# A transformer layer with routed experts on one core: all stages rewritten (stacked heads in 64 rows, four buffers a ring, weighted sums on TensorE)

## The reference

```
qkv  = x @ w_qkv                      # 16 heads of 8 numbers each
attn = softmax(causal(q k^T / sqrt(8))) @ v
a    = layernorm(attn @ w_proj + b_proj + x) * gamma + beta
x2   = layernorm(x + a)
p    = softmax(x2 @ gate_w^T); the best 2 of 14 experts, weights p0/(p0+p1), p1/(p0+p1)
moe  = w0 * expert_i0(x2) + w1 * expert_i1(x2)    # expert: gelu(x2 w1 + b1) w2 + b2, 128 -> 256 -> 128
out  = layernorm(x2 + clip(x2 + moe, -100, 100))
```

## Time and profile before

| what | us |
|---|---|
| median of 3 runs (lowest, highest) | 615.03 (613.7, 618.78) |
| span of the profiled execution | 603.8 |
| busy: PE, PEld | 408.8, 311.8 |
| busy: DVE, ACT, POOL | 334.4, 289.7, 329.2 |
| instructions | 13418 |

### The profile page before, as it was taken

One profiled execution on the slowest core, in us unless ns is written; L12 is line 12 of the kernel. 1 busy time (PEld: TensorE's weight loads), 2 busy tenths in 40 slices (PEclk: granted clock), 3 DMA queues, 4 the chain that ended last, 5 costly groups with the idle time before them and its releaser, 6 DMA issues.

```text
span 603.8 us, 13418 instructions
## 1 busy us (share of the span) xinstructions
PE 408.8 (68%) x3651; PEld 311.8 (52%) x3651; DVE 334.4 (55%) x1238; ACT 289.7 (48%) x670; POOL 329.2 (55%) x460
## 2 busy tenths in 40 slices
PE   3178998679779669789879678315778877874000
PEld 2045676557557447556657455214757766863000
DVE  3355687467557557567658554443445444442893
ACT  2015576465466455465546456214444544542563
POOL 3803355475466464465566567642656555553793
PEclk9989999798798798798888889557898889898555
DMA  2658773454354362453363210252222222221462
GB/s 59 68 93 191 149 120 54 61 73 54 53 73 58 49 79 38 60 66 57 66 72 42 41 33 19 82 152 60 70 67 75 66 73 68 77 64 43 140 175 69
DMA packets 78121, 45.39 MB, mean 75 GB/s; under 512 B 11217, under 2 KB 76003, under 8 KB 78076
## 3 DMA queue, kind: packets, MB, share of 16 engines
q1 hardware_dynamic: 72668, 35.22, 33.4%
q0 software_dynamic: 4544, 8.44, 5.0%
q10 hardware_dynamic: 864, 1.19, 0.7%
HBM read 18.61 MB, written 14.28 MB: 54 GB/s over the span
## 4 chain that ended last, share of the span: by engine, by line
SPq 27%; PE 23%; DMA 22%; issue 12%; DVE 8%; ACT 3%; POOL 3%; another core or an unknown queue 0%; POOLq 0%; ACTq 0%; DVEq 0%
DMA k_stack<-part_l 18%; SPq L475 16%; PE M L1140 5%; SPq L507 5%; PE M L1143 3%; PE G L1189 2%; PE M L1325 2%; PE S L1109 2%; SPq L501 2%; PE S L1318 2%; DMA rows<-sorted_rows 2%; DVE row_max L831 1%; DVE probs L1062 1%; DVE stats L1072 1%; PE S L1119 1%
## 5 line engine op out<-in xcount | busy, mean ns | idle before, releaser
L831 DVE TENSOR_REDUCE row_max<-M 128x2 f32<-128x512 f32 (+1 forms) x192 | 129.1, 679 | 88.0 <-PE M L1143 87.4
L676 ACT ACTIVATE probs<-S 128x768 f32<-128x768 f32 x128 | 103.4, 809 | 80.9 <-PE S L1119 70.6
L1140 PE MATMUL M<-k_stack,q_stack 96*128 96x256 bf16 (+1 forms) x512 | 85.9, 279 | 64.3 <-DMA k_stack<-part_l 61.1
L637 POOL DMA_INDIRECT results<-y_rows x78 | 79.8, 1023 | 66.6 <-DVE y_rows L1052 41.1
L1140 PEld LDWEIGHTS M<-k_stack,q_stack 96*128 96x128 bf16 x512 | 44.9, 110 | 84.0 <-DMA k_stack<-part_l 56.2
L583 POOL TENSOR_SCALAR_AFFINE_SELECT probs<-probs 128x256 f32<-128x256 f32 x128 | 49.2, 408 | 67.6 <-ACT probs L676 66.7
L627 POOL DMA_INDIRECT sorted_rows<-x,row_no x64 | 63.2, 987 | 28.0 <-issue 20.7
L1143 PE MATMUL M<-causal_neg,ident_bf 128*128 128x256 bf16 (+1 forms) x192 | 68.2, 355 | 0.0
L1325 PE MATMUL M<-probs,hT 128*128 128x128 f32 x312 | 55.3, 305 | 14.3 <-ACT hT L758 7.2
L758 ACT ACTIVATE hT<-S,probs 128x128 f32<-128x128 f32 x156 | 51.3, 369 | 24.1 <-PE S L1318 19.8
L1318 PE MATMUL S<-rows_t,probs 128*128 128x128 f32 x312 | 57.4, 313 | 0.5 <-ACT rows_t L752 0.2
(11 more groups left out here) (166 smaller groups left out, 795.3 us busy)
## 6 DMA issues: line engine op xcount, KB each, us to landing
rows<-sorted_rows SPq DMA_DIRECT2D x78, 64.5 KB
q_stack<-part_h SPq DMA_DIRECT2D x48, 64.0 KB
k_stack<-part_h SPq DMA_DIRECT2D x48, 64.0 KB
xin<-in_L_attn_target_dram SPq DMA_DIRECT2D x16, 128.0 KB, 3.3
q_stack<-part_m SPq DMA_DIRECT2D x32, 64.0 KB
k_stack<-part_m SPq DMA_DIRECT2D x32, 64.0 KB
xres<-in_L_attn_target_dram SPq DMA_DIRECT2D x16, 128.0 KB, 3.2
q_stack<-results SPq DMA_DIRECT2D x8, 256.0 KB, 3.1
```

Of the source, the lines that this page charges most:

```text
L637: pool.indirect_dma_start(results, bass.IndirectOffsetOnAxis(ap=y_rows[:, q, D:ROW].bitcast(U32), axis=0), y_rows[:, q, 0:D], None, bounds ...
L676: act.activation(probs[:, n], S[n % 2][:, 0:3 * T], ACT.Exp, scale=SCALE).then_inc(exp_done, 1)
L831: dve.tensor_reduce(row_max[:, (r - 1) % 3, h0:h0 + nh, half], M[i % 2][:, :].rearrange("p (h k) -> p h k", h=nh), X, ALU.max).then_inc(m_ ...
L1140: pe.matmul(bank[:, j * keys:j * keys + keys], q_stack[0:SHIFT, b, h0 + j, half * P:half * P + P], k_stack[0:SHIFT, b, h0 + j, 0:keys], st ...
```

## The change

- **Stacks.** Two heads share one slot: one in rows 0 to 63, one in rows 64 to 127 (`TILE` = 64), so 8 slots instead of 16. A part goes to every 8th partition, 16 in all. Matmuls of scores and maxima have 64 rows; the two halves of the array write different PSUM banks, in alternation for scores, unit by unit for maxima. The masks are matmuls of 64 rows too, two per former one, of half the columns each. The shift rows are set to zero by two more DMAs a step and written by two instead of one.
- **Order of the body.** Rings of 4 instead of 3, everything from the maxima on lies one step further behind (maxima for t - 2, scores t - 3, ..., scatter t - 6), 22 steps instead of 21, all written out. `early` is t < 3, where ACT issues the DMAs of k. The first four loads of x stand at the start, the expert weights at t = 4, 5, 6. The shift's turn stands earlier in unit 7.
- **Routing in fewer operations.** One comparison instead of two, no copies of logits, indices and best values, the region's offset added by the rank matmuls, one sum less; the mean's sign and the epsilon of the two layer norms go from DVE to POOL (4 small operations a step).
- **Experts.** All 78 tiles written out with constant counts. Layer 1 is two tiles behind, layer 2 four, bias and scatter five; 3 buffers for turned rows and hidden values, 10 for results. ACT also makes 64 diagonal matrices of the weights, one a tile from tile 6 on.
- **Last stage.** PE puts x2 into 8 PSUM banks (8 matmuls of 512 columns) and adds the weighted results with 8 matmuls of 128 columns a chunk. All 16 loads are issued at once, from rows that lie side by side (2 KB instead of 512 B). DVE's clip reads PSUM; the negative mean's product goes to POOL.

The diff, cut to its core:

```diff
-    SHIFT = 96
+    TILE = P // 2
+    SHIFT = 6
+    R = 4
+    HR = 3
+    YR = 10
...
         def run(eng, body):
-            for t in range(FIRST):
-                body(t, t % 3, t // 3)
-            with eng.Fori(0, (LAST - FIRST) // 3) as i:
...
+            for t in range(B + 6):
+                body(t, t % R, t // R)
...
         def s_unit(t, u):
-            return (t - 2, u - 2) if u >= 2 else (t - 3, u + NP - 2)
+            return (t - 3, u - 2) if u >= 2 else (t - 4, u + NP - 2)
...
# SP, body
-                        for stack, part, which, places in parts:
-                            for n in places:
-                                sp.dma_start(stack[HD * n:HD * n + HD, r], part[:, r, which]).then_inc(stacked[r], 16)
+                    after(sp, s_ready, NP * (t + 1 - R))
+                        for a in range(2):
+                            sp.dma_start(q_stack[TILE * a + SHIFT:TILE * a + SHIFT + 2, r],
+                                         zeros_bf[0:2, None, :].broadcast_to([2, NP, T])).then_inc(stacked[r], 16)
+                    sp.wait_ge(h_split, t + 1)
+                    for n in (0, 1, 3):
+                        sp.dma_start(q_stack[n:P:HD, r], part_h[:, r, 0]).then_inc(stacked[r], 16)
...
+                    for w in range(2):
+                        sp.dma_start(q_stack[SHIFT + w:P:TILE, b], shift_t[w * 2 * NP * TT:(w + 1) * 2 * NP * TT, b]).then_inc(shifted, 16)
...
# PE, scores
-                for j in range(2):
-                    h = 2 * n + j
-                    pe.matmul(S[n % 2][:, j * T:j * T + T], k_stack[:, b, h, 0:P], q_stack[:, b, h, :],
...
+                for half, at, nq in ((0, 0, T), (1, T, P)):
+                    for a in range(2):
+                        rows = slice(TILE * a, TILE * a + TILE)
+                        last = pe.matmul(S[n % 2][:, 512 * a + at:512 * a + at + nq], k_stack[rows, b, n, half * P:half * P + P],
+                                         q_stack[rows, b, n, T - nq:T], start=(half == 0), stop=True, skip_group_check=True)
...
# PE, maxima
+                rows = slice(TILE * a, TILE * a + TILE)
+                bank = M[a]
+                for j in range(ng):
+                    pe.matmul(bank[:, j * keys:j * keys + keys], q_stack[rows, b, g0 + j, half * P:half * P + P],
+                              k_stack[rows, b, g0 + j, 0:keys], start=(j == 0), stop=False, skip_group_check=True)
+                for c in range(2):
...
+                    last = pe.matmul(diag, mask_m[rows, c], ident_fold[rows, None, :].broadcast_to([TILE, ng, TILE]), start=False,
...
# experts
         def run_tiles(eng, body):
+            for s in range(TILES + 5):
                 body(s, s % XR, s // XR)
...
+                if 0 <= n < 2 * NT:
+                    act.activation(diag[:, n], ident[:, :], ACT.Copy, scale=wgt[:, n // 2, n % 2:n % 2 + 1]).then_inc(diag_done, 1)
...
# PE, last stage
+                pe.matmul(acc[c][:, :], ident[:, :], x2_all[:, bass.ts(c, 2), :].rearrange("p b n -> p (b n)"), start=True, stop=False,
...
+                pe.wait_ge(got_in[c], 32)
+                for i in range(CH):
+                    n = CH * c + i
+                    for k in range(2):
+                        last = pe.matmul(acc[c][:, i * D:i * D + D], diag[:, 2 * n + k], got[k][:, n], start=False, stop=(k == 1),
+                                         skip_group_check=True)
+                last.then_inc(acc_done, 1)
```

More of the change, by code:

```diff
@@ L525, in store @@
                 sp.dma_start(out_chunks[c], fin[:, half]).then_inc(out_sent[half], 16)
[L527 removed]
+            run_chunks(sp, (4, store))
             for half in range(2):
@@ L557, in more_constants, with zero_keys @@
+            def zero_keys(some):
+                for i in some:
+                    pool.memset(zeroed(k_stack[:, i]), 0).then_inc(keys_zeroed[i], 1)
+            def more_constants():
                 pool.memset(v_aug[:, :, :, :, HD:32], 0.0).then_inc(consts_p, 1)
@@ new lines, in _ @@
+            for q in range(XR):
+                dve.memset(expert_unit[:, q:q + 1], float(1 << EXPERT_BITS * q)).then_inc(numbered, 1)
+            for q in range(2):
+                dve.memset(block_unit[:, q:q + 1], float(1 << BLOCK_BITS * q)).then_inc(numbered, 1)
+            dve.memset(zeroed(q_stack[:, 1]), 0).then_inc(queries_zeroed[1], 1)
+            dve.wait_ge(consts, 4)
+            for a in range(2):
+                part = slice(TILE * a, TILE * a + TILE)
+                dve.tensor_copy(ident_fold[part, :], ident_bf[part, part]).then_inc(folded, 1)
@@ new lines, in _, with masks_below @@
+            dve.wait_ge(wqk_in, 16)
+            for a in range(2):
+                last = dve.tensor_copy(wqk[:, :, D // 2 * a:D // 2 * a + D // 2].rearrange("p w (d g) -> p w d g", d=HD),
+                                       wqk_raw[:, 0:2 * D].rearrange("p (w g a d) -> p w a d g", w=2, g=NP, a=2)[:, :, a])
+            last.then_inc(consts_v, 1)
+            for i in range(2, R):
+                dve.memset(zeroed(q_stack[:, i]), 0).then_inc(queries_zeroed[i], 1)
+            def masks_below():
+                dve.wait_ge(masks, 8)
+                rows = slice(TILE, P)
+                dve.tensor_copy(mask_m[rows], mask_m1[rows]).then_inc(folded, 1)
+                dve.tensor_copy(mask_s[rows], mask_s1[rows]).then_inc(folded, 1)
+                dve.wait_ge(gate_turned, 1)
+                dve.tensor_copy(gate_t[:, :], M[0][:, 0:E]).then_inc(consts_v, 1)
@@ L1111, in scores @@
[L1111 to L1120 removed]
+                    pe.wait_ge(shifted, 32 * (s + 1))
@@ new lines, in scores @@
+                if n % 2:
+                    for c in range(2):
+                        for a in range(2):
+                            rows = slice(TILE * a, TILE * a + TILE)
+                            diag = S[n % 2][:, 512 * a:512 * a + 2 * T].rearrange("p (k q) -> p k q", k=2)[:, :, TILE * c:TILE * c + TILE]
+                            last = pe.matmul(diag, mask_s[rows, c], ident_fold[rows, None, :].broadcast_to([TILE, 2, TILE]), start=False,
+                                             stop=True, skip_group_check=True)
@@ L1226, in body @@
-                    if u == 2 and isinstance(t, int) and t == B + 3:
+                        if t == 0:
+                            pe.wait_ge(weights_in, 80)
+                            pe.transpose(M[0][:, 0:E], gate_raw[:, :], ident[0:E, 0:E]).then_inc(gate_turned, 1)
+                    if u == 2 and on(t) and not early(t):
+                        project(t, r)
+                    for i in m_units(u) if on(t - 2) else ():
+                        if i == 2 and on(t) and not early(t):
+                            turn_x(t, r, lap)
+                        maxima(t, r, i)
@@ L1228, in body @@
+                    if u == 2 and t == B + 4:
                         pe.wait_ge(seen_done, B)
                         pe.wait_ge(y_ready, B)
[L1230 to L1234 removed]
+                        pe.matmul(G[:, 0:E], ones_bf[:, :], seen[(B - 1) % 2], start=True, stop=True).then_inc(counts_ready, 1)
```

884 lines of the change are left out of this document (443 added, 441 removed).

## The result

The changed kernel takes 535.93 us (median of 4 runs, 531.87 to 541.66), the kernel before 614.37 in the same comparison: a ratio of 0.875, 95% interval 0.866 to 0.884. Forecast were 510, range 478 to 548. The profiled execution took 531.87 us, with a span of 530.1. Medians are of all executions; a ratio with an interval leaves out those that took over 1.5% more than the same kernel's fastest.

A forecast was written before the change was run, and what follows sets the result against it. The prediction took attention to be bound by a loop in which PE waits for the stack DMAs, with PE the next bound. Attention 339, experts 122 and last stage 38 gave 499 us, with 11.2 more 510; range 478 to 548.

The forecast's parts named there:

- (a): Attention: rings of 4 and one step more between stacks and maxima remove the wait of 4.5 us a step.
- (b): Attention's stack DMAs to 16 partitions instead of 8: between 4.3 and 12.9 us a step, nothing gained in steady steps.
- (c): Attention's scores in two halves of 64 rows: 0 to 1.8 us a step saved, taken as cancelling with (d).
- (d): PE's changes of shape in attention, 21 instead of 8: 0 to 2.6 us a step lost, cancelling with (c).
- (e): POOL in attention: 15.3 us a step, not binding a 17 us step but the floor if PE gets faster.
- (f): DVE in attention, 14.3 us busy a step, loses ten of its smallest operations; nothing comes of it.
- (g): Start of attention: first maxima at 22 us, t = 3 at 32, t = 5 at 62, t = 17 at 266.
- (h): Drain from the step of the last maxima to the first expert tile: 72.7 us again, attention ending at 339.
- Rival D: Experts' stage: SP's 0.69 us gaps stay in written-out tiles; 1.8 us a tile, 23 us more, 533; chance 0.12.
- B: Attention: halves overlap, shape changes are free, POOL's 15.3 us bounds the step; 20 us less, 490; chance 0.15.
- A: Attention: shape changes drain, halves don't overlap; a step of 19.5 us, 30 us more, 540; chance 0.12.
- C: Attention: the loop only moves, to shift rows behind the stack DMAs; 20 us a step, 36 more, 546; chance 0.08.

The follow-up runs named there:

- a_no_slack: Changed kernel whose first maxima also wait for the stack DMAs issued one step before, so without the extra step of slack; 490.24 us on a quiet chip.
- after_third: Profile of the changed kernel unaltered, on a quiet chip; 482.96 us against 576.08 for the kernel before, ratio 0.845.
- b_plain_pool: Kernel before with its 78 expert tiles written out and POOL's indirect scatter of results replaced by plain DMAs; 559.18 us against 614.03, with pauses.
- b_tiles_out: Kernel before with its 78 expert tiles written out with constant counts, nothing else changed; 577.8 us against 578.04 on a quiet chip.
- a_narrow: Changed kernel with each middle- and low-part stack DMA split into two of 8 partitions from t = 4 on; 563.25 us with pauses, changed kernel 527.87.

## Why the prediction came out as it did

The time lay in the range and 26 us above the forecast; one term, the experts' stage, carries most of that.

- **(a), (b), the loop: right in effect, wrong in which half does it.** The wait of 4.5 us a step went, and the clock came back with it. But (a) gave the credit to the slack and counted the quicker write as hidden. a_no_slack shows that the slack isn't needed, and its landing of at most 2.6 us after the issue, against 6.5, says why. No run has slow writes on a quiet chip, so what the slack alone would have given stays open. By the rule that the prediction cited for (b) (the Trainium skill, DMA: Bandwidth & Descriptors, "Why a DMA increments its semaphore by 16 and not by 1") the number of DMA engines at work on a transfer doubles; the trace agrees as to the rate, 61 GB/s became 124 to 126, and no run here shows which engines worked.
- **(c), (d), halves and changes of shape: right, and both can be read.** In after_third (162 to 225 us) a unit of scores takes 0.18 us from its first matmul to the next unit's, where the kernel before took 0.33: 1.2 us a step of the 1.8 that were possible. The two halves start within 0.01 us of each other, in whatever order they are issued. A change of shape costs 0.09 us: a mask of 64 rows and 128 columns is followed by its like after 0.056 us, by a matmul of another shape that doesn't wait after 0.146. The 13 changes more are 1.2 us, not 2.6, so the two do cancel. PE is busy 15.0 to 15.5 us in a step at full clock, 0.6 to 1.0 less than the 16.05 of before; the masks of half the columns may be the rest.
- **The step: 17.0 forecast, 17.97 measured on the first chip, 15.82 on a quiet one.** What is on top are 1 to 2 us of pause and, in some steps, the lower clock behind a standstill of PE (0.84 in the step of 18.6 us above, where PE had stood for most of 206 to 207.5 us; the two of 16.7 us have 1.00). I had read the low clock of before as a consequence of the DMA wait alone.
- **(e) POOL's floor, (f) DVE: right.** POOL is busy 13.7 of 15.7 us; my 15.3 without its 1.4 of issue gaps is 13.9. DVE is busy 12.3, and neither binds.
- **(g) start: 3 us late.** By the first maxima of a step, the mark that the prediction used: 20.3 (22 forecast), t = 3 at 34.7 for 32, t = 5 at 65.2 for 62, t = 17 at 274.4 for 266. So 3 us come from the start and 5 from twelve steps of 17.43.
- **(h) drain: near.** From 274.4 to 349.6 it is 75.2 us for 72.7, the last 2.5 of the 11.
- **Experts: the step that failed.** The mis-sized term is 78 x 1.5 + 5 = 122 us; it measured 142.6, or 1.83 a tile with the lag in it. I read SP's 0.69 us pieces as time that SP spent on registers, so that constants and deeper rings would take part of them away. They go with the pauses: with all counts constant there were 43 of them instead of 41, on quiet chips there are none, and b_plain_pool, which leaves SP's code as b_tiles_out has it, has 2. Without them the floor is POOL's scatter, near the 1.4 that I gave, and old and new kernel both already stand on it: 111.6 and 111.7 us. The earlier trace rows could have said so: 58.6 us of scatters and 20.4 of gaps behind them are 79 of 100 us, more than any other engine had, and only 22.4 were a wait for DVE. Rival D (0.12) had the place and the size, 1.8 us a tile and 533 us, and its sign came, SP pieces as many as now; its reason was wrong, since the gaps don't stay because of what SP reads.
- **Last stage: right, with POOL as its bound.** 37.9 us for 38 (39.2 from the first load of results), one chunk every 2.8 us for 3.0. The power costs 1.02 and not 1.27, but my own terms, 1.307 + 1.272 + 0.2, make 2.8 and not 3.0. The chain that ended last runs through DVE, which stands almost nowhere. Yet POOL's order is what closes on itself:

```profile
512.17 0.20 POOL L695 TENSOR_TENSOR minus_mean<-neg_mean,rstd 128x4 f32<-128x4 f32 x1
512.32 1.26 POOL L687 TENSOR_TENSOR x_all<-probs,x_all 128x512 f32<-128x512 f32 x1
513.82 1.02 POOL L693 TENSOR_TENSOR rstd<-var_eps,minus_half 128x4 f32<-128x4 f32 x1 [0.24 <-DVE var_eps L1132]
```

```profile
512.75 0.86 DVE L1131 TENSOR_SCALAR neg_mean<-moments 128x4 f32<-128x4 f32 x1
520.71 0.17 DVE L1131 TENSOR_SCALAR neg_mean<-moments 128x4 f32<-128x4 f32 x1
```

POOL's addition, power and product take 2.5 of the 2.8 us. The 0.24 before the power is a wait for DVE, and DVE is late by its sign: 0.80 to 0.86 us in the six chunks in which POOL's addition runs beside it (it ends within 0.03 us of the addition, 513.61 and 513.58), 0.17 in the two where it is over. Without that DVE's five operations would take some 2.1 us a chunk, an estimate. No run takes one of the two engines' work away, so this is read and not tested.
- **Rivals.** B had the quiet chip's outcome for the size (490) and not the mechanism: PE, not POOL, is what ends the step. A's price for a change of shape was twice too high, and the halves do overlap. C, E and F are ruled out by the waits above, in which PE waits for no q_stack<-shift_t and no k_stack. The 5.4 us between span and median that came back are luck: the 11.2 in the sum was not a cost of the kernel.

No kernel here that does the whole work is measurably faster than the changed one. The next gain would be in the results' scatter: 22 us on a quiet chip, 53 on one with pauses.

## What to carry to other kernels

Before you count an engine's gaps as its own, see whether the semaphore updates around them are late: where one comes 2 us after its instruction's end, and on several engines in the same stretch, an edit to the engine that waits won't remove the gap. When a stage has no busy engine, ask which engine's instruction starts as soon as its predecessor's gap is over (here POOL's scatter, 0.94 + 0.34 us), and test the floor by replacing that one operation; four runs did here what no count of gaps could. The chain can run through an engine that is merely never idle: look whether its instructions are stretched by a neighbour's. And where a change both shortens a transfer and adds slack for it, find out which of the two does the work: undo them one at a time, and where the chip itself disturbs, on an undisturbed one.

## What the runs showed of the hardware that I had not expected

- The same kernel takes 614 us on one chip and 576 to 579 on others. The pauses (waits of up to 3.4 us for work that is done, in a_narrow 3.9, SP's trifles at 0.70 us) appear only on the first and only where POOL's indirect scatters run; with plain DMAs from POOL in their place they are gone from the stage. On the quiet chips the same scatters run without any. What makes them is open.
- DVE's copy of 642 elements with a register address takes 602 ns under the new experts' stage, where the kernel before had 505; without the scatter it is 498. Single copies take 0.50 or 0.72 to 0.74 us; why is open:

```profile
L1098 DVE COPY probs<-experts 128x642 f32 x58 | 34.9, 602 | 17.7 <-DVE y_rows L1107 10.3 <-issue 7.4
```

```profile
L1097 DVE COPY probs<-experts 128x642 f32 x57 | 28.4, 498 | 16.4 <-DVE y_rows L1106 16.4
```

- A plain DMA of the same 64 KB from POOL holds it 598 ns, the indirect one 1003 to 1028, and 0.3 more between two.
- DVE's sign change of 128x4 numbers takes 0.17 us by itself and 0.80 to 0.86 beside POOL's addition of 128x512, with which it ends.
- A change between matmuls of 64, 32 or 128 rows and columns costs PE 0.09 us from start to start; one between 96 and 128 rows, in the kernel before, costs nothing (0.109 us, as without it).
